# An attention and FFN block: the exponentials' biases moved from POOL to DVE, with new instruction lists

## What is computed

```python
def _L0_attn_ref(x, Wqkv, Wo):
    qkv = (x @ Wqkv).reshape(B, S, 3, H, HD)
    ...
    scores = jnp.einsum('bhqd,bhkd->bhqk', q, k) * HD ** (-0.5)
    scores = jnp.where(causal, scores, jnp.float32(-1000000000.0))
    a = jax.nn.softmax(scores, axis=-1)
    o = jnp.einsum('bhqk,bhkd->bhqd', a, v)
    ...
    return o @ Wo
...
# ternary_quant(w): s = mean(|w|); clip(round(w / s), -1, 1) * s
g = jax.nn.silu(x @ w1q.T) * (x @ w3q.T)
ffn = g @ w2q.T
...
x = x + _L0_attn_ref(_layernorm(x), L0_attn_Wqkv, L0_attn_Wo)
x = x + _L0_ffn_ref(_layernorm(x), L0_ffn_w1, L0_ffn_w3, L0_ffn_w2)
```

## Time and profile before

| | us |
|---|---|
| median of 3 runs | 583.4 (581.24 to 584.58) |
| profiled execution, device time | 579.74 |
| its span | 578.0 |
| around the span | 1.7 |
| PE / DVE / POOL / ACT busy | 498.8 / 424.9 / 370.6 / 331.5 |

### The profile page before, as it was taken

The page is one execution under the profiler, slowest core; times in us unless marked ns, Lnnn a source line. Parts: engine busy times, 40 slices in busy tenths (PEclk is TensorE's granted clock), DMA queues, the critical chain, the costliest instruction groups (busy, mean ns, idle before and its releaser), DMA issues. The chain is left out here.

```text
span 578.0 us, 11518 instructions
## 1 busy us (share of the span) xinstructions
PE 498.8 (86%) x4092; PEld 230.4 (40%) x4092; DVE 424.9 (74%) x1058; ACT 331.5 (57%) x833; POOL 370.6 (64%) x461
## 2 busy tenths in 40 slices
PE   2658835767997999999999998999999999939997
PEld 2223412232443444544444444444444444414443
DVE  7697878877988798876898986887789883524321
ACT  4878866876765767655357876653477663013320
POOL 3096898866977787865686898673669783322320
PEclk9698975688998999999999999999999999969999
DMA  8729999999689959586568576956583747240001
GB/s 326 266 78 218 180 192 213 207 253 193 132 135 136 182 72 185 75 164 135 137 111 168 93 137 92 199 140 127 92 168 72 144 76 160 80 89 2 0 1 73
DMA packets 224206, 79.52 MB, mean 138 GB/s; under 512 B 213226, under 2 KB 213226, under 8 KB 224148
## 3 DMA queue, kind: packets, MB, share of 16 engines
q1 hardware_dynamic: 224148, 78.79, 66.3%
HBM read 20.97 MB, written 4.19 MB: 44 GB/s over the span
## 5 line engine op out<-in xcount | busy, mean ns | idle before, releaser
L673 POOL TENSOR_TENSOR early<-early 128x512 f16<-128x512 f32 (+1 forms) x192 | 194.7, 1023 | 45.3 <-DVE early L1005 32.2
L781 ACT ACTIVATE early<-early,exp_bias 128x512 f32<-128x512 f32 (+3 forms) x256 | 140.9, 552 | 72.2 <-POOL exp_bias L680 72.1
L1145 PE MATMUL work<-late,w_ternary 128*128 128x512 f16 (+1 forms) x704 | 159.3, 383 | 12.3 <-DMA late<-rows 11.3
L993 DVE CUSTOM_DVE_ANT_0 early<-score_bank,mask,scalars 128x512 f32<-128x512 f32 (+3 forms) x256 | 132.7, 543 | 24.7 <-POOL early L673 16.7
L1005 DVE CAST early<-early 128x512 f16<-128x512 f32 (+1 forms) x148 | 97.8, 675 | 21.7 <-ACT early L781 10.4
L1145 PEld LDWEIGHTS work<-late,w_ternary 128*128 128x128 f16 (+1 forms) x704 | 68.4, 100 | 95.6 <-issue 18.1
L1145 PE MATMUL work<-xt,wqkv_hi 128*128 128x512 f16 x256 | 81.3, 401 | 6.4 <-DMA xt<-rows 4.3
L1308 PE MATMUL work<-w_ternary,late 128*128 128x512 f16 (+1 forms) x352 | 78.1, 379 | 0.2 <-DVE late L1041 0.2
L698 POOL TENSOR_TENSOR late<-late 128x512 f16<-128x512 f32 (+1 forms) x44 | 52.2, 1186 | 37.9 <-ACT late L818 37.0
L811 ACT ACTIVATE late<-work,scalars 128x512 f32<-128x512 f32 (+1 forms) x44 | 29.9, 679 | 40.0 <-PE work L1145 26.3
L1145 PE MATMUL work<-xt,wqkv_lo 128*128 128x512 f16 x128 | 50.8, 397 | 0.0
(11 more groups left out here) (108 smaller groups left out, 718.3 us busy)
## 6 DMA issues: line engine op xcount, KB each, us to landing
rows<-in_L_attn_x SPq DMA_DIRECT2D x16, 256.0 KB, 3.0
x_res<-in_L_attn_x SPq DMA_DIRECT2D x12, 256.0 KB, 3.0
out_y<-x_res SPq DMA_DIRECT2D x12, 256.0 KB, 2.4
late<-in_L_ffn_w SPq DMA_DIRECT2D x4, 682.5 KB, 5.0
early<-in_L_ffn_w SPq DMA_DIRECT2D x3, 768.0 KB, 12.2
late<-in_L_ffn_w SPq DMA_DIRECT2D x3, 768.0 KB, 6.3
late<-in_L_attn_Wqkv SPq DMA_DIRECT2D x4, 512.0 KB, 6.4
late<-in_L_attn_Wqkv SPq DMA_DIRECT2D x1, 1024.0 KB, 9.8
```

The source lines that it names most:

```text
L673: pool.tensor_tensor(split_view(s, p, 1, h), raw_view(s, p, h), split_view(s, p, 0, h), ALU.subtract).then_inc(low_done, 1)
L781: last = act.activation(piece, piece, ACT.Exp, bias=bias, accum_out=sums[:, s % 2, at:at + 1])
L993: last = dve.tensor_tensor_reduce(raws[n % RAWS][:, off:off + cols], score_bank[h][:, off:off + cols], mask[:, S - cols:S], scalar(exp_sca ...
L1145: last = pe.matmul(bank, lhs, rhs, start=(n == 0), stop=(n == len(terms) - 1))
```

## The change

Every step keeps what it computes, and its operands. The 96 `bias` steps are taken out of POOL's list and put into DVE's, where each stands behind the second maximum of its pair, directly (36 of them) or up to four steps further on; the function moves with them, from `pool.wait_ge` and `pool.tensor_scalar` to `dve.wait_ge` and `dve.tensor_scalar`. The set of high halves on ACT and on DVE is the same as before (44 and 148). All five lists are laid in a new order. The parts of the diff that the prediction speaks of:

```diff
@@ -79,176 +79,171 @@
     "sp": """
-        x_load:1,0-1 weight_load:w3,0-2 weight_turn:w1,1 weight_turn:w1,0 weight_load:w3,3 weight_turn:w1,2
-        probs_turn:0,0-2 res_load:0,3 xt:1,0-1 x_load:1,2 weight_load:w2,0 probs_turn:1,0 x_load:1,3 probs_turn:1,1
...
-        weight_turn:w3,0 res_load:0,1 probs_turn:3,0-2 weight_turn:w2,0-1 probs_turn:4,0-1 weight_turn:w2,2-3
-        yt:0,0-1 probs_turn:4,2 yt:0,2-3 xt:2,0-1 x_load:2,2-3 probs_turn:5,0-2 xt:2,2-3 x_load:3,0 probs_turn:6,0
...
+        weight_turn:w1,0-1 x_load:1,0 weight_load:w3,0 res_load:0,2 weight_load:w3,1 weight_turn:w1,2
+        weight_load:w3,2 x_load:1,1 weight_load:w3,3 probs_turn:0,0-2 weight_load:w2,0 xt:1,0 weight_load:w2,1
...
+        res_load:0,0 probs_turn:3,0-2 res_load:0,1 weight_turn:w2,2 weight_turn:w2,1 weight_turn:w2,0 probs_turn:4,0
+        weight_turn:w2,3 yt:0,0-1 probs_turn:4,1 yt:0,2-3 xt:2,0-1 x_load:2,2 probs_turn:4,2 x_load:2,3 xt:2,2
...
     "pool": """
-        stats_x:0,0-3 weight_round:w1,0 stats_x:1,0 weight_round:w1,1-6 bias:0,0,1 weight_round:w1,7 bias:0,0,3
-        weight_round:w1,8-9 low:0,0,0 weight_round:w1,10 low:0,0,1 stats_x:1,1 bias:0,1,1 low:0,0,2-3 xt:1,0
...
+        stats_x:0,0-3 weight_round:w1,0-10 low:0,0,0-1 stats_x:1,0 low:0,0,2-3 low:0,1,0-3 xt:1,0 weight_round:w3,0
...
     "act": """
-        norm_x:0,0-2 xt:0,1 norm_x:0,3 xt:0,0 xt:0,3 xt:0,2 weight_sum:w1,0 split:0 weight_sum:w1,1 split:1
...
+        norm_x:0,0-3 xt:0,0 weight_sum:w1,0 xt:0,2 weight_sum:w1,1 split:0 xt:0,1 xt:0,3 weight_sum:w1,2 split:1
+        weight_sum:w1,3 split:2-3 split:8 weight_ternary:w1,0-1 split:4 weight_ternary:w1,2 q:0 split:5
...
     "dve": """
...
...
     "pe": """
-        xt:0,1 xt:0,0 xt:0,2-3 top_turn:qk top_turn:v q:0 weight_mean:w1 k:0-1 scores:0,0 q:1 scores:0,1 top_turn:wo
...
-        values:2 q:5 scores:3,2 weight_mean:w2 scores:4,0 q:6 k:6 inverse:3 scores:4,1 values:3 v:1,0-2 scores:4,2
-        project:0,0-2 scores:5,0 project:0,3 v:1,3 k:7 scores:5,1 inverse:4 q:7 values:4 gate:0,0 lin:0,0 gate:0,1
...
-        scores:15,0 gate:2,7 lin:2,7 gate:2,8 lin:2,8 scores:15,1 inverse:14 gate:2,9-10 lin:2,9 values:14 lin:2,10
-        scores:15,2 down:2,0-1 inverse:15 down:2,2 values:15 down:2,3 project:3,0-3 gate:3,0-1 lin:3,0-1 gate:3,2-3
...
+        top_turn:qk xt:0,0-3 top_turn:v weight_mean:w1 q:0 k:0 top_turn:wo k:1 scores:0,0 k:2 q:1 scores:0,1 v:0,0-1
...
+        values:2 scores:3,2 scores:4,0 k:6 inverse:3 scores:4,1 q:6 values:3 v:1,0-1 project:0,0 scores:4,2
+        project:0,1-3 v:1,2 scores:5,0 v:1,3 q:7 k:7 gate:0,0 inverse:4 lin:0,0 gate:0,1 lin:0,1 scores:5,1 gate:0,2
...
+        gate:2,5 lin:2,5 scores:15,0 gate:2,6 lin:2,6 gate:2,7 inverse:14 scores:15,1 lin:2,7 gate:2,8 values:14
+        scores:15,2 lin:2,8 gate:2,9-10 lin:2,9-10 inverse:15 down:2,0 values:15 down:2,1 project:3,0-3 down:2,2-3
+        gate:3,0-1 lin:3,0-1 gate:3,2-3 lin:3,2 gate:3,4 lin:3,3-4 gate:3,5-6 lin:3,5-6 gate:3,7-8 lin:3,7-8
...
@@ -673,13 +668,6 @@
-            def bias(s, p, h):
-
-                both = slice(piece_columns(p, h - 1).start, piece_columns(p, h).stop)
-                pool.wait_ge(score_free, place(s, p, h) + 1)
-                pool.tensor_scalar(exp_bias[:, (NF * s + p) % 2, both], row_max[:, (NF * s + p) % 2, both], -1.0, LOG_UNIT,
-                                   ALU.mult, ALU.add).then_inc(bias_made, 1)
-
...
@@ -995,6 +981,13 @@
+            def bias(s, p, h):
+
+                both = slice(piece_columns(p, h - 1).start, piece_columns(p, h).stop)
+                dve.wait_ge(score_free, place(s, p, h) + 1)
+                dve.tensor_scalar(exp_bias[:, (NF * s + p) % 2, both], row_max[:, (NF * s + p) % 2, both], -1.0, LOG_UNIT,
+                                  ALU.mult, ALU.add).then_inc(bias_made, 1)
+
```

More of the change, by code:

```diff
@@ L103 @@
[L103 to L112, removed]
@@ L175 @@
+        lin:2,8 exp:15,2,1 high:15,2,0 exp:15,2,2 high:15,2,1 exp:15,2,3 high:15,2,2 lin:2,9 high:15,2,3 gate:2,10
+        lin:2,10 inverse:15 ot:15 yt:3,0-3 gate:3,0-1 lin:3,0 gate:3,2-3 lin:3,1 gate:3,4 lin:3,2-4 gate:3,5 lin:3,5
+        gate:3,6-8 lin:3,6-7 gate:3,9 lin:3,8 gate:3,10 lin:3,9-10
     """,
     "dve": """
-        pad:w1 stats_x:0,0-3 top_part:0-2 xt:0,1 top_part:3 xt:0,2 xt:0,0 top_turn:qk top_v xt:0,3 split:0
-        top_turn:v split:1-2 stats_x:1,0 split:3 weight_mean:w1 split:8 q:0 k:0 split:4 stats_x:1,1 max:0,0,0
@@ new lines @@
+        lin:1,6 values:9 high:10,1,1-2 max:10,2,0-1 bias:10,2,1 high:10,1,3 gate:1,7 lin:1,7 max:10,2,2-3
+        bias:10,2,3 gate:1,8 lin:1,8 max:11,0,0 inverse:10 max:11,0,1 bias:11,0,1 k:13 max:11,0,2 high:11,0,0
+        max:11,0,3 gate:1,9 bias:11,0,3 high:11,0,1 lin:1,9 high:11,0,2 max:11,1,0 high:11,0,3 max:11,1,1 gate:1,10
+        bias:11,1,1 max:11,1,2 lin:1,10 max:11,1,3 high:11,1,0 bias:11,1,3 high:11,1,1-3 values:10 max:11,2,0-1
+        bias:11,2,1 q:13 max:11,2,2-3 bias:11,2,3 down:1,0 max:12,0,0 inverse:11 max:12,0,1 bias:12,0,1 max:12,0,2-3
@@ new lines @@
+        max:14,2,1 bias:14,2,1 lin:2,4 max:14,2,2-3 k:15 bias:14,2,3 gate:2,5 lin:2,5 max:15,0,0-1 inverse:14
+        bias:15,0,1 max:15,0,2 gate:2,6 max:15,0,3 high:15,0,0 bias:15,0,3 lin:2,6 high:15,0,1-2 max:15,1,0 gate:2,7
+        high:15,0,3 max:15,1,1 lin:2,7 bias:15,1,1 max:15,1,2-3 bias:15,1,3 high:15,1,0 gate:2,8 high:15,1,1
+        values:14 high:15,1,2 max:15,2,0 lin:2,8 high:15,1,3 max:15,2,1 bias:15,2,1 max:15,2,2 gate:2,9 max:15,2,3
+        bias:15,2,3 lin:2,9 inverse:15 gate:2,10 lin:2,10 down:2,0 values:15 project:3,0 down:2,1 stats_y:3,0
@@ L229 @@
+        project:3,1 stats_y:3,1 norm_y:3,0-1 project:3,2 stats_y:3,2 project:3,3 stats_y:3,3 norm_y:3,2-3 down:2,2
+        gate:3,0 down:2,3 lin:3,0 gate:3,1 lin:3,1 gate:3,2 lin:3,2 gate:3,3 lin:3,3 gate:3,4 lin:3,4 gate:3,5
+        lin:3,5 gate:3,6 lin:3,6 gate:3,7 lin:3,7 gate:3,8 lin:3,8 gate:3,9 lin:3,9 gate:3,10 lin:3,10 down:3,0-3
     """,
     "pe": """
-        xt:0,1 xt:0,0 xt:0,2-3 top_turn:qk top_turn:v q:0 weight_mean:w1 k:0-1 scores:0,0 q:1 scores:0,1 top_turn:wo
-        v:0,0-1 scores:0,2 k:2 v:0,2 q:3 weight_mean:w3 scores:1,0 v:0,3 q:2 scores:1,1 inverse:0 k:3 values:0
```

269 lines of the change are left out of this document (130 added, 139 removed).

## The result

| | before | after |
|---|---|---|
| median, us | 582.75 (581.24 to 584.58, 4 runs) | 574.70 (574.58 to 575.15, 4 runs) |
| profiled execution, us | 579.74 | 574.75 |
| its span, us | 578.0 | 573.0 |

The ratio is 0.986, with a 95% interval of 0.983 to 0.989: the change makes the kernel 8.05 us faster by the medians. The two profiled executions differ by only 5.0 us, because the one of before lies 3.0 us under its median and the one of after lies at its own. The forecast was 11.8 us.

What follows compares the result with a forecast made beforehand. PE was taken as the bound from 184 to 505 us, full DMA before, and a hole near the end. Gains 8.3 + 6 - 2.5 = 11.8 us gave 571.5 us from 583.4; forecast band 565 to 577, range 560 to 583.

Steps and rivals of the forecast that it cites:

- the hole: PE's 10.52 us wait after project:3,3; down:2,2 and down:2,3 moved behind the projections fill it, gaining 9.5 us.
- the turns of w1: Opening: weight_turn:w1,0-1 first in SP's list use DMA's empty stretch, so the DMA chain starts earlier; 4 us gain.
- part 3: The 96 biases moved from POOL to DVE: PE's stalls in 184 to 460 us rise, -2.5 us, ends 0 and -12.
- Part 1: End of the lists: two down steps moved behind the projections; 9.5 + 1.8 - 3.0 = 8.3 us gain.
- the last slot: Before values:15: less PE work covers slot 15's chain, so the stall grows to 3.7 us, a loss of 3.0 us.
- the slow clock behind it: The 3.6 us after project:3,3's wait at granted clock 0.50; full clock there gains 1.8 us.
- Part 2: The opening, up to the first FFN: earlier DMA chain and new step order give 6 us, ends -3 and 11.
- the order around the first gate: gate:0,0 ahead of inverse:4, yt ahead of probs_turn:4,1: PE's 3.84 us wait may go; 2 us gain.
- The price of one bias: Each bias on DVE takes 0.43 us because it stands while POOL subtracts; 41 us in all for 96.
- Rival 3: DVE becomes the bound, each bias waiting for a whole POOL subtraction (1.13 us); slower, 594 us; chance 0.10.
- A term booked at nothing: POOL loses 96 bias instructions, some 22 us; no gain booked, since ACT's idle time costs nothing while PE is full.

Runs made afterwards that it cites:

- the two other kernels with the same end: After's kernel with weight_turn:w1,0-1 behind the first two w3 loads, 578.34 us; after's kernel with inverse:4 ahead of gate:0,0, 576.74 us.
- by columns: After's kernel with each bias on DVE made as two or four one-column instructions (256 instead of 96): 567.99 us, ratio 0.976.
- the end of after behind the old lists: The kernel before up to 418 us, then all five lists in after's order, biases on POOL throughout: 587.67 us, ratio 1.009.
- the opening alone: After's lists up to 175.5 us, then those of before, with gate:0,0 behind values:4 again: 580.02 us, ratio 0.995.

## Why the prediction was right, and where it was not

The time lies in the range and on the forecast's side; it is 3.2 us above the forecast by the medians (574.7 for 571.5). Of the mechanisms behind it only the hole and the turns of w1 were right as they were told. In the opening two errors nearly cancel, and in part 3 one term was mis-sized and one booked at nothing. So the sum is right in part by luck.

**Part 1, the hole: right.** 9.5 us were forecast and 9.8 measured; the slow clock behind it 1.8 and 1.9, with the granted clock at full level behind 512.45 us. The page of after has 9 in every slice of the clock there.

**Part 1, the last slot: right in size, wrong in mechanism.** Forecast were 3.0 us more at `values:15`; it was 4.0 us (5.3 in the two other kernels with the same end), spread over five waits of which `values:15` is the smallest. The working measured cover from `scores:15,2` on, as if that step came on time. It does not. From the start of `scores:15,0` to `values:15` it takes 34.6 us before, 33.4 in after, 34.6 with only the down steps moved and 32.6 by columns: in these four the slot's chain through maxima, exponentials, halves and four raw buffers needs nearly the same time whatever PE has between, and PE's steps only decide where the rest of the wait is met. It is no fixed length: with the end of after behind the old lists it takes 40.6 us. Between the two steps PE has, apart from the slots' own steps, eight up steps and three down steps before (29.0 us), eight and two with only the down steps moved (24.1), ten and one in after (22.8). So after has no more cover there than the kernel with only the down steps moved, and loses as much ahead of `values:15`. What it does better stands behind: it starts `scores:15,0` two up steps earlier among the FFN's steps, and with these it can leave `down:2,1` behind `values:15`, where it covers the chain of the halves (2.85 us where it is missing). And its waits are short and spread, with no matmul at the low clock behind them. That is the difference between 10.2 us lost and 4.8. The prediction counted these steps, but not that the gain of the hole hangs on them: the hole's 11.7 us belong to the new lists as a whole, not to the two down steps, and not to the new end alone, which was slower behind the old lists.

**Part 2: right in its sum, by two errors that nearly cancel.** The turns of w1 were priced at 4 us and the order around the first gate at 2; the sum of 6 stands against 4.9 in the trace. But only 0.8 us of it come ahead of `values:3`, where the turns must show, and 4.1 between `values:3` and `gate:0,0`, where the order must. The turns do work as foreseen: put back, they cost 3.6 us by the medians, 2.5 of it ahead of `values:3`. What the prediction missed is that the rest of the new opening takes some 1.6 us of this back. It booked nothing for the biases of slots 0 to 4 on DVE, and by columns, where they no longer stand, `values:3` starts 4.2 us earlier (140.8 us) and `gate:0,0` 3.1. The order was under-sized: moving `inverse:4` alone is worth 1 us by the trace and 2.0 by the medians, and no run takes the rest of it apart. `gate:0,0` came at 175.8 us (forecast 177), with `scores:5,1`, `inverse:4` and `values:4` now behind it. Without the first gate's order and with the biases' cost in it, the opening alone was worth only 2 us.

**Part 3: the step that failed.** The price of one bias was right (398 ns for 430). DVE's work in the middle rose by less than forecast (to 235.8 of 276 us, 85%, not 92%): the 60 biases take 25.2 us there, but the float16 copies 8 less (46.0 us for 54.2; their mean fell from 675 to 590 ns), and some other steps fall outside this stretch now. And yet PE lost 7.7 us more in the middle instead of 2.5 (busy 265.4 of 276 us, 96%, where over 97% was to be seen). The step "the banks come 0.4 us later, so PE's stalls go from 4.5 to 7" went from DVE's load to PE's stalls, and load was the wrong measure. What counts is whether a long bias, one that meets an instruction of POOL (36 of 96), stands ahead of a step of DVE for which PE waits; one such place is shown above, the others were not followed one by one. Of the 7.7 us, 4.4 go when the bias can no longer stand (7.6 to 3.2 in the traces); about 3.3 us stay, from the new lists or from the short instructions' own time on DVE. The bounds given, 0 and 12, did hold it. Rival 3 had the right mechanism, a bias that waits for a POOL subtraction, with the wrong way of costing: it priced 60 biases at the longest and asked for DVE to be full, while the median bias was 169 ns and DVE had 40 us idle. (Its sum has 4.5 us for slots 1 to 4 where 27 less 22.2 gives 4.8; its 594 stays.)

**A term booked at nothing.** That POOL loses 22 us of work was given no gain of its own. The wide bias on DVE beats the bias on POOL in the same lists by only 1.9 us, which the intervals leave open, and this looks like a confirmation. But it is the balance of two larger terms: by columns, where no bias stands, these lists are 8.6 us faster than with the biases on POOL (7.4 by the ratios), and the standing takes 6.7 of it back (5.7). In the old lists the same comparison gives 1.6 to 1.9 us. The 8.6 hold for the place that the biases were given in POOL's list, and another might cost less.

The sum by the traces: forecast 8.3 + 6 - 2.5 = 11.8; measured 7.7 (9.8 + 1.9 - 4.0) + 4.9 - 7.7 = 4.9 us.

**What stays open.** What causes the 3.3 us that stay in the middle; which steps of the order around the first gate bring its 4.1 us; why the end of after does so badly behind the old lists, since that kernel changed two things; and how much of the 2.0 us of moving `inverse:4` is noise.

## What to carry to other kernels

Before a filler is moved into a hole, take it out of its old place alone: here that run gave nothing, because the two down steps were the cover of a chain some 34 us long. In after, whose lists start this chain earlier and keep one down step behind `values:15`, the move paid; with the same end behind the old lists it did not. A small instruction is priced by what stands behind it and by its longest occurrences, not by its mean times its count. When a move between two engines measures as nothing, look whether a gain on one and a cost on the other cancel. Where a narrow instruction on DVE is seen to stretch beside POOL's, cutting it into one-column instructions may be faster though there are more of them.

## What of the hardware was unexpected

- An instruction of two or four columns on DVE, 151 ns at its shortest, stood up to 2232 ns beside POOL, and each of the 36 that took over 250 ns ended 23 to 30 ns after an instruction of POOL. One of one column was never over 154 ns in 256 occurrences (156 in the 256 of the old lists), 105 of them inside a POOL subtraction, and four in a row took 0.32 us.
- The granted clock fell behind short waits already: to 0.56 behind 5.48 us of idle PE and to 0.55 behind 2.85 us, near the lower of its two levels (1.2 for 2.4 GHz), and it was at 1.00 again within 4 us. In after, waits of 1.52 and 0.62 us in the same place left it at full level.
